# A graph layer's 65 edge steps in one loop with one window width, column sums a step behind, and another order on GpSimd

## What is computed

```python
agg = jax.ops.segment_sum(edge_attr, col, num_segments=x.shape[0])
h = jnp.concatenate([x, agg, u[batch]], axis=1)   # batch is all zero
h = jax.nn.relu(h @ W1 + b1)
h = h @ W2 + b2
x = _layernorm(x + h, axis=-1)                    # (x - m) / sqrt(v + 1e-5)
```

## Time and profile before

| | us |
|---|---|
| median of 3 runs | 275.75 (275.32 to 275.93) |
| profiled execution | 276.12 |
| its span | 274.4 |
| PE busy | 213.2 (78%) |
| DVE busy | 177.2 (65%) |
| ACT busy | 50.8 (19%) |
| POOL busy | 41.5 (15%) |
| moved by DMA | 110.06 MB, 401 GB/s over the span |

### The profile page before, as it was taken

One profiled execution on the slowest core, in us unless ns is written; L12 is line 12 of the kernel. 1 busy time (PEld: TensorE's weight loads), 2 busy tenths in 40 slices (PEclk: granted clock), 3 DMA queues, 4 the chain that ended last, 5 costly groups with the idle time before them and its releaser, 6 DMA issues.

```text
span 274.4 us, 15313 instructions
## 1 busy us (share of the span) xinstructions
PE 213.2 (78%) x6767; PEld 168.7 (61%) x6767; DVE 177.2 (65%) x435; ACT 50.8 (19%) x100; POOL 41.5 (15%) x49
## 2 busy tenths in 40 slices
PE   0874899987886449999884789895898897867872
PEld 0763687855655347877653658674766676655751
DVE  7842285793674997596874436959928769465542
ACT  0410122311211201122210211322022212121210
POOL 6400020030210012040300200300303003030020
PEclk9998699999999859999999599999599999999997
DMA  7999999999999999999999999999999999999994
GB/s 252 391 396 401 400 401 404 402 401 405 402 406 402 401 402 402 404 401 415 416 418 409 416 412 414 421 415 416 418 426 428 422 425 432 418 430 422 429 393 174
DMA packets 28863, 110.06 MB, mean 401 GB/s; under 512 B 2008, under 2 KB 3374, under 8 KB 26926
## 3 DMA queue, kind: packets, MB, share of 16 engines
q1 hardware_dynamic: 25588, 105.83, 95.9%
q10 hardware_dynamic: 3258, 4.00, 4.0%
HBM read 106.63 MB, written 3.20 MB: 400 GB/s over the span
## 4 chain that ended last, share of the span: by engine, by line
PE 58%; issue 13%; DVE 12%; DMA 12%; POOL 1%; ACT 1%; DVEq 1%; POOLq 0%; ACTq 0%
PE rows_ps L860 31%; PE cols_ps L872 14%; DMA slots<-in_edge_attr 12%; PE hid_ps L904 4%; PE hid_ps L886 3%; DVE tall_ids L687 3%; PE hid_ps L895 3%; PE hid_ps L880 2%; ACT rows L444 1%; DVE hot L615 1%; DVE z L678 1%; DVE first_of_pair L570 1%; POOL rstd L408 1%; DVE dst_local L583 1%; DVE high L696 1%
## 5 line engine op out<-in xcount | busy, mean ns | idle before, releaser
L860 PE MATMUL rows_ps<-slots,hot 64*32 64x128 f32 x6240 | 113.4, 285 | 35.7 <-issue 23.4
L860 PEld LDWEIGHTS rows_ps<-slots,hot 64*32 64x32 f32 x6240 | 93.6, 110 | 53.5 <-issue 50.7
L641 DVE TENSOR_TENSOR agg_t<-agg_t,cols_ps 128x128 f32 (+1 forms) x65 | 21.5, 331 | 84.1 <-PE cols_ps L872 83.8
L872 PE MATMUL cols_ps<-row_hot,rows 128*128 128x128 f32 (+1 forms) x260 | 56.3, 341 | 11.4 <-ACT rows L444 6.3
L615 DVE TENSOR_TENSOR hot<-edge_node,iota 128x768 f32<-128x768 f32 x65 | 61.8, 952 | 2.5 <-issue 1.6
L444 ACT ACTIVATE rows<-rows_ps 128x256 f32<-128x256 f32 x65 | 25.0, 384 | 177.3 <-PE rows_ps L860 170.1
L872 PEld LDWEIGHTS cols_ps<-row_hot,rows 128*128 128x128 f32 x260 | 40.8, 198 | 25.3 <-ACT rows L444 13.1
L408 POOL TENSOR_TENSOR rstd<-var_eps,minus_half 128x4 f32<-128x4 f32 (+1 forms) x13 | 16.6, 1275 | 196.7 <-DVE var_eps L672 196.7
L631 DVE TENSOR_TENSOR row_hot<-row_node,iota 128x256 f32<-128x256 f32 (+1 forms) x65 | 38.4, 591 | 0.0
L399 POOL TENSOR_TENSOR z<-x_rows,b_all 128x512 f32<-128x512 f32 (+1 forms) x13 | 17.2, 1323 | 29.8 <-PE hid_ps L880 29.8
L678 DVE TENSOR_SCALAR z<-z,moments,rstd (+1 forms) x49 | 17.2, 410 | 1.1 <-POOL rstd L408 1.0
(11 more groups left out here) (119 smaller groups left out, 70.3 us busy)
## 6 DMA issues: line engine op xcount, KB each, us to landing
slots<-in_edge_attr SPq DMA_DIRECT2D x65, 1536.0 KB, 14.9
x_rows<-in_x ACTq DMA_DIRECT2D x11, 256.0 KB
out<-z SPq DMA_DIRECT2D x11, 256.0 KB
dst_int<-in_dst SPq DMA_DIRECT2D x1, 384.0 KB, 3.9
dst_int<-in_dst ACTq DMA_DIRECT2D x1, 384.0 KB, 4.6
x_rows<-in_x ACTq DMA_DIRECT2D x1, 192.0 KB
out<-z SPq DMA_DIRECT2D x1, 192.0 KB
rest_slot<-in_edge_attr ACTq DMA_DIRECT2D x1, 128.0 KB, 8.5
```

The source lines that it names most:

```text
L641: V.tensor_tensor(cols, cols, cols_ps[:, 0:n], ALU.add).then_inc(added, 1)
L860: done = T.matmul(rows_ps[i][c * SPAN:(c + 1) * SPAN, h, 0:feats], hot[j][part, c * RUN + r, :], slots[part, j, c, r * feats:(r + 1) * fea ...
L872: done = T.matmul(cols_ps[:, 0:n], rows[i][:, h, :], row_hot[j][:, h, 0:n], start=(h == 0), stop=(h == HALVES - 1))
```

## The change

- **One loop on PE and DVE.** `sparse_lap` and `dense_lap` are replaced by `one_lap`, which PE runs 13 times; DVE has steps 0 to 3 ahead of its loop and runs it 12 times. Level 2 of step t-1 comes behind level 1 of step t in all laps, except that level 2 of step 3 of a lap stands ahead of level 1 of step 4.
- **One width.** `row_hot`, level 2 and `add` have 224 columns in all steps; level 2 and `add` of the very last step have 128.
- **PSUM.** Level 1 uses two pairs of banks (`SETS = (0, 1, 0, 1, 1)`). The transposes get `turn_bank`, the second layer `y_bank`, and `hid_ps` keeps the first layer. `turn_x` no longer waits for `z_made`; `product2` does.
- **Where a place's work stands.** x is transposed in step 1 of a lap instead of step 3 or 4; the first layer's product with x follows in step 2 of the same lap; the product with the sums stands in step 1 of the next, `product2` in step 2. ACT issues the load of x in step 3 instead of step 4.
- **GpSimd** runs `bias_add` of place i+1 ahead of `reciprocal_deviation` of place i. It also clears `x_rows` once at the start.
- **Places.** The blocks now start at node 128, and the place with the 106 odd nodes comes first instead of last but one. Transfers and bytes are the same in sum.
- PE's 384-column product in lap 12 and PE's wait for `plan_made` are gone. DVE copies the count of bad ids (`bad_total`) in lap 9 in a new wait ahead of an `add`.

```diff
-SETS = (0, 1, 0, 1, 2)
-DENSE_LAP = 6
-DENSE = DENSE_LAP * LAP
+SETS = (0, 1, 0, 1, 1)
+DENSE = 6 * LAP
...
@@ gpsimd
+            G.memset(x_rows[:, :, :], 0.0).then_inc(x_zero, 1)
...
             bias_add(0, 0)
+            bias_add(1, 1)
             for i in range(places):
                 reciprocal_deviation(i, i)
-                if i + 1 < places:
-                    bias_add(i + 1, i + 1)
+                if i + 2 < places:
+                    bias_add(i + 2, i + 2)
...
@@ scalar
                 for j in range(LAP):
                     t = lap * LAP + j
-                    if dense_lap:
+                    if t:
                         copy_rows(t)
-                    elif t + 1 < DENSE:
-                        copy_rows(t + 1)
-                    if j == 0 and lap:
-                        relu(lap - 1)
-                    elif j == 3:
+                    if j == 1:
+                        if lap:
+                            relu(lap - 1)
                         copy_x(lap)
-                    elif j == 4 and lap < final:
+                    elif j == 3 and lap < final:
                         load_x(lap + 1)
...
@@ vector
-            sparse_lap(0)
-            with dve.Fori(1, DENSE_LAP) as lap:
-                sparse_lap(lap)
+            first_at = step_bases(0, LAP - 1)
+            for t in range(LAP - 1):
+                add(t, first_at[t], COLS)
+                make_hot(t + AHEAD, t + AHEAD)
+            dve.wait_ge(wide_ids_copied, SHARE)
...
-            with dve.Fori(DENSE_LAP, laps) as lap:
-                dense_lap(lap)
+            with dve.Fori(1, laps) as lap:
+                one_lap(lap)
+            add(held, 0, DENSE_COLS)
...
@@ tensor
+            def one_lap(lap):
                 counts(lap)
                 for j in range(LAP):
                     t = lap * LAP + j
                     if j == 4:
+                        level2(t - 1, j - 1, COLS)
                     level1(t, lap, j)
                     if j == 0:
+                        with pe.If(lap > 0):
+                            level2(t - 1, LAP - 1, COLS)
+                        with pe.If(lap < 1):
+                            first_products()
+                    elif j == 1:
+                        with pe.If(lap > 0):
+                            pe.wait_ge(added, lap * LAP + 1)
+                            product1_agg(lap - 1, start_of(lap - 1))
...
+                        level2(t - 1, j - 1, COLS)
+                        turn_x(lap, lap * 16 + x_landed(0, 0))
+                    elif j == 2:
+                        with pe.If(lap > 0):
+                            product2(lap - 1, lap - 1)
+                        level2(t - 1, j - 1, COLS)
+                        product1_x(lap, BLOCK)
                     elif j == 3:
+                        level2(t - 1, j - 1, COLS)
...
-            with pe.Fori(0, DENSE_LAP) as lap:
-                sparse_lap(lap)
-            level2(DENSE - 1, LAP - 1, False)
-            with pe.Fori(DENSE_LAP, laps) as lap:
-                dense_lap(lap)
+            with pe.Fori(0, laps) as lap:
+                one_lap(lap)
+            level2(held, LAP - 1, DENSE_COLS)
```

244 lines of the change are left out of this document (84 added, 160 removed).

## The result

The changed kernel takes 278.6 us where the kernel before takes 275.4 us (medians of five). One of its five executions took 287.28 us at a mean granted clock of 0.82 and is left out of the ratio, which is 1.0101 with a 95% interval of 1.0080 to 1.0122: 1.0% slower. Forecast were 274.4 us and a range of 273.6 to 276.1. The profiled execution of the changed kernel took 278.01 us with a span of 276.3; the one of before 276.12 with 274.4. So 1.9 us are to be found within the span; what lies around it is 1.7 us in both. The profiled execution is the quickest of the five: the medians lie further apart, and that part is in no trace of these two.

What follows compares the result with a forecast made beforehand. The prediction took the DMA stream of loads to bound the kernel until 265.3 us, then a 9.1 us tail. Only the stream's -1.3 counted, all else zero: 275.75 - 1.3 = 274.45, said as 274.4 us, range 273.6 to 276.1.

Steps and rivals of the forecast that it cites:

- the stream: Loads until step 64 lands: without the second loop body's code packets, the last landing comes 1.3 us earlier.
- the width: 224 columns in all steps: longer DVE and PE work lies beside the stream and costs nothing.
- the tail: From the last load's landing to the span's end, 9.1 us: same operations and store bytes, so zero change.
- the ninth: 16 KB code packet at 177 to 179 us: fell on an already late DMA engine, delaying step 64 by 1.3 us.
- 4 x 0.3: Level 2 in the tail at half clock: at most 1.2 us longer, part of rival 2.
- Level 2 a step later: PE in dense laps: no longer waits for ACT's copy, 6.3 us of idle time; worth nothing while data are late.
- The hole in lap 3: PE idle while DVE transposes ids, now a step earlier: a similar hole as before, costing nothing.
- GpSimd and ACT: GpSimd's sum goes first, so ACT's 7.1 us of copy waits behind the load of x go; worth nothing in time.
- the new waits: `product2` waits for the previous place's addition, DVE in lap 9 for PE's three tiny products: both cost nothing.
- Rival 2: Tail: without the 384-column product PE's clock falls to half ahead of the last level 1; 276.8 us, chance 0.07.
- Rival 3: Each lap of the one long loop fetches its code again: 278.3 us or more, chance 0.04.
- rival 4: Stream beyond step 30: the DMA rate hangs on the width and stays at 402 GB/s; 278.6 us, chance 0.04.

Runs made afterwards that it cites:

- e0_after: The changed kernel once more, unchanged, for a second trace: 278.4 us, ratio 1.0146 to the kernel before.
- e7_before_long_general: The kernel before with VectorE's never-run general path lengthened from 135 to 215 instructions by waits never executed: 277.43 us, ratio 1.0059.
- e4_before_224: The kernel before with 224 columns in every step instead of 128 from step 30 on: 280.54 us, ratio 1.0195.
- e10_narrow_short_pad: The changed kernel with 128 columns everywhere (incomplete sum), VectorE's general path shortened to 86 instructions, 16 padding instructions: 276.47 us, ratio 1.0016.

## Why the prediction was wrong

The steps that failed are three terms of the sum: the 1.3 us for the stream, which measured 0 to 0.5, and two terms put at nothing, the width (1.1 us at the last level 1) and the tail (1.4 us).

**The stream (forecast -1.3; -0.5 in the first trace, 0 in the second).** The count was right, or one too high: four packets from 18.7 to 40.3 us, one in the tail, none from 137 to 157 us, none in each lap, and the ninth of before is gone too. The term was mis-sized, because its reading (a packet costs the last engine time that it never makes up, and the end lands later by it) does not hold. The prediction's own sign of being wrong, a landing at 265.3 with fewer packets, is what `e0_after` shows. In the three traces with the two old bodies and ten packets (before, `e7_before_long_general`, `e4_before_224`) load 64 lands at 265.3, 265.1 and 265.1; in the thirteen with one body, and five or six packets, at 264.8 to 265.3. Part of the forecast gain can be seen on the way. The three loads from step 41 to 44, forecast at about 12 us, take 11.3 in all traces with one body, against 13.3, 12.5 and 12.9 with two; some 0.6 of this is the load of x, which has moved: from step 34 to 37 the changed kernel takes 12.0 us, before it was 11.3. But the same two bodies with the ninth packet at 179.3 us give 12.5 in `e7_before_long_general`, so even the 13.3 was in part that one execution. From step 30 to step 64 the last engine's landings span 132.1, 132.1 and 131.6 us with two bodies and 130.8 to 131.6 with one. Fewer packets, or what else came with them, are worth 0 to 1.3 us there, 0.6 between the means. It is lost ahead of it: load 30 lands at 133.1 to 133.5 with two bodies, at 133.4 to 134.2 with one. Why, no run shows.

**224 columns (forecast 0; +1.1).** This is the step that failed most. The rule was that width comes out only where a step takes longer than 3.8 us. It was checked on the laps below step 30 alone, where PE may be behind its data: in the middle of the kernel lateness is free, as long as the stock lasts. In the last lap the steps do take longer, 3.9, 4.2 and 4.1 us, and there nothing makes up for it. From level 1 of step 61 (253.79) to that of step 64 (266.03) PE takes 12.2 us, without a pause but the 0.7 for the add, for data that come in 11.2 (three steps of 3.74, by the landings of steps 60 and 64 at 249.9 and 264.8). Four column sums lie in it, each some 0.3 us longer than with 128 columns: 1.2 us, the whole lateness. The prediction had the sum that would have said so ("4 x 0.3"), but used it for the clock only. On DVE the term was too small as well: `row_hot` took 14.0 us more (52.5 against 38.5), not 4.0, since 12 of the 65 ran beside GpSimd.

**Level 2 a step later (forecast 0).** "Worth nothing while data are late" does not fit: in the old order the width costs 4.8 us, in the new one less. How much of this is level 2 and how much the rest of the new order was not separated.

**The hole in lap 3 (forecast: cost nothing).** It costs the mean of the engines 0.3 us and in `e0_after` 1.1, but neither the landing of load 30 nor the time shows it. Before, DVE's transposes left PE without hot matrices; now they also hold up an add ahead of a column sum ahead of level 1.

**The tail (forecast 0; +1.4).** "The same operations" was true, and the chain to the store was the same to 0.1 us. But the two waits behind the store depend on where VectorE's code lies, 1.0 us for the packet inside the store and 0.3 to 0.4 for the jump. The prediction weighed where packets of code fall in the stream, and never asked what the same queue does during the last store, where one engine of 16 is the whole wait.

**GpSimd and ACT, the new waits (forecast 0).** Right: ACT's wait of the earlier trace rows is gone, and of the new waits named there none shows at the end. But GpSimd's sum now falls beside DVE's `row_hot` in nearly every lap. It takes 1862 ns in the mean, before 1323, and the 12 `row_hot` beside it take 1.64 us in the mean (before, 11 of both widths, 1.00), the other 53 take 0.62, together 808 ns:

```profile
82.41 1.72 DVE L624 TENSOR_TENSOR row_hot<-row_node,iota 128x448 f32<-128x448 f32 x1
```

**The rivals.** Rival 2 named the place, the tail, and the sign, and came nearer in time (276.8), by luck: its mechanism is wrong, the clock was 1.00 from 248 to 270 us. Rival 3 has no packets, rival 4 no lower rate (411 to 431 GB/s beyond step 30, but for the last two slices). Chances of 0.15 for slower were too few for a change that lengthens 35 steps on both engines that stand in the last chain.

## What to carry to other kernels

When a kernel is bound by its stream, price added work not by the average slack but in the last lap: write down, between two fixed starts there, the work of the engine that ends last and the time in which data come; before, PE's pauses there made 1.8 us of 10.9. Then look at what stands behind the last store, where code that is never executed can cost: a jump over a long fallback took 2.5 us in place of 0.5, and one 8 KB packet of code inside the last store made the wait for it 1.0 us longer. A change that shortens or lengthens VectorE's program moved both here, so a difference of a microsecond between two kernels may be nothing but this; a few waits as padding tell. And take a second trace before a gain of half a microsecond is believed: the first one here had it, the second did not.

## What the runs showed of the hardware

- VectorE's jump over 135 instructions took 0.55 us in one program and 2.5 in the other; over 86 instructions 0.2, over 215 instructions 2.95.
- In seven traces an 8 KB code packet falls among the 512-byte packets of the last, 64 KB store, and one engine's part lands 0.9 to 1.2 us after the other fifteen; the packet itself takes 0.5 to 0.7 us. In the nine traces without it the last part lands 0.01 to 0.4 us behind.
- The last landing of the stream hardly moves with the spread of the engines: 265.1 and 265.3 us with the first engine at 262.9 (`e7_before_long_general`) and 261.7 (before).
- Where `row_hot` on DVE and the sum on GpSimd ran at the same time both took longer: in the changed kernel `row_hot` 1.64 us in place of 0.62 in the mean (one 1.72 us, at 82.41), GpSimd's sum some 2.02 us in place of 1.3.
- In `e10_narrow_short_pad` the granted clock was half (1.2 of 2.4 GHz) from 251.0 to 257.8 us, shortly after PE had waited 2.21 us for data; level 1 took 2.25 and 2.82 us in place of 1.58, and that of step 64 came 1.6 us behind its data.
